# Softmax denominators of an attention kernel: four one-column fp32 matmuls replaced by two rounded 512-column matmuls and a diagonal pick, with the finish moved from tile 10 to tile 14

## The chip, the cores and the metric

The kernel runs on one core of one Trainium2 chip. The metric is the device time of one execution in microseconds (us), lower is better.

## The reference

Layer 0 is group norm and one-head self-attention over the 4096 pixels of each of 4 images with 128 channels, layer 1 a causal token attention and an 8-expert feed-forward. The change is in layer 0:

```python
    x: (4, 128, 64, 64)
    h = group_norm(x, norm_w, norm_b)                 # 32 groups
    q, k, v = h @ Wq + bq, h @ Wk + bk, h @ Wv + bv   # per pixel, 128 channels
    scores = jnp.einsum('bnc,bmc->bnm', qf, kf) * C ** (-0.5)   # N = 4096
    attn = jax.nn.softmax(scores, axis=-1)
    o = jnp.einsum('bnm,bmc->bnc', attn, vf)
    return x + (o @ Wo + bo)
```

Everything is fp32. The layer 1 part (token layer norm, a running softmax over 8 heads, top-2 of 8 experts) isn't touched.

## The kernel before

`softmax_attention` does layer 0. The queries are cut into 32 blocks of 512 (8 for each of 4 images), the keys of an image into 32 tiles of 128. The loop counter g runs over 32 x 32 = 1024 tiles: n is the block, t the tile in it, b the image and i = n % 8 the block in the image. Every engine has its own instruction stream, written out in program order; semaphores alone tie them together. For each tile TensorE computes the transposed scores of 128 keys by 512 queries (L374 to L376, three matmuls on operands split into a rounded high part and a rounded rest, type fp32r), the row scores that serve for maxima of a block 36 tiles ahead (`row_scores`, L359), and the weighted values of the tile three back (`weigh`, L388 to L390). ScalarE takes the exponential (L497, `pf`) and rounds it (L502, `p_hi`); GpSimd subtracts (`low`, L224, `p_lo`); VectorE takes maxima (L632) and adds the exponentials of a block up (L648, `sum_ps`, and the last into `den`, L652).

The sum over the 128 partitions of `den` is what the change is about. `denominators(n - 1)` is issued by TensorE at the end of the iteration t = 2 of the next block (t = 1 where i = 6): four plain fp32 matmuls, with a 128-column piece of `den` as the weights and one column of ones as the moving operand, into four columns of the shared bank `pj_ps`. VectorE's `inverse` (L657) takes the reciprocal of 128x4 values an iteration later, SyncE sends them to DRAM and back as a row broadcast over the partitions (`rb_sb`), and VectorE's `finish` (L665, L669) multiplies and adds at t = 10.

```python
for i in range(QT):
    mm = pe.matmul(pj_ps[:, i:i + 1], den[:, i * C:(i + 1) * C], ones[:, 0:1], start=True, stop=True)
mm.then_inc(den_pe, 1)
```

The bank `pj_ps` also takes the projections: `project_q` (once a block, t = 21 or 22), `project_k` for the next image (i = 6, at t = 3, 7, ..., 31), read by ScalarE's `hold_k` and VectorE's `difference` (L614 to L618) one iteration later; `project_v` (i = 7 from t = 8 on every fourth, and i = 0 at t = 0 and 4), read by `high_v` and `low_v` (L624). `key_low` (L218) on GpSimd follows at i = 7 from t = 6 on and at i = 0, t = 2. Blocks with i = 5 hold the group statistics of the next image: `channel_moments` (VectorE, t = 10), `group_means` (TensorE L257, t = 12), `group_variance` (t = 13), `scale_shift` (L697 to L701, t = 15). Block W_AT = 26 holds `weight_sums` (L705) at t = 5, 10, 15, 20 and `center_weights` (L711) one later each. Row scores stop with the block 30, t = 28.

## Time and profile before

| | |
|---|---|
| Time, median of 3 runs | 2730.43 us (2727.93 to 2730.92) |
| Time of the profiled execution | 2731.85 us, span 2730.1 us |
| TensorE busy | 2560.8 us, 94% |
| VectorE busy | 2154.0 us, 79% |
| GpSimd busy | 2059.8 us, 75% |
| ScalarE busy | 1841.1 us, 67% |
| Attention over the 32 blocks | about 65 us to 1850 us, the rest is layer 1 |
| `denominators` (L405) | 31 between 131.5 us and 1799.1 us, and a last one at 1846.8 us |

A busy TensorE isn't TensorE at its peak, since matmuls overlap in this profile: a 512-column matmul is shown as 0.39 us long, and the next one starts about 0.23 us after it. So the distance between starts is what counts. Plain fp32 matmuls show as two records each.

### The profile page before, as it was taken

To read this page: it belongs to the slowest core of one execution; us is meant where nothing else is said; L and a number is where in the kernel's file an instruction comes from. 1 tells how busy PE (TensorE), PEld (TensorE's weight loads), DVE (VectorE), ACT (ScalarE), POOL (GpSimd) and SP (SyncE) were. 2 spreads that over 40 slices of the span, in tenths; PEclk is the share of its full clock that TensorE was granted. 3 is DMA by queue.
4 is the path that set the end of the run, shared out by engine and by line. 5 is a ranking of instruction groups with operands and counts; after the bars stand their busy time and mean duration, and the time that the engine had idled before them with its cause. 6 is when DMAs were issued, how large, how long until landed. Compare 5 with 4: busy or idle time off the path is not lost. (4 is left out here: it accounts for less than half of the span.)

```text
span 2730.1 us, 37025 instructions
## 1 busy us (share of the span) xinstructions
PE 2560.8 (94%) x10851; PEld 1859.4 (68%) x10851; DVE 2154.0 (79%) x3225; ACT 1841.1 (67%) x3375; POOL 2059.8 (75%) x1688
## 2 busy tenths in 40 slices
PE   6999999999999999999999999996979999998868
PEld 2788877788887788887778888773445555555433
DVE  4788887788887788888778888861888988988984
ACT  3666777667667676667766666775877767766640
POOL 3677776777776777777677777782559989989995
PEclk7999999999999999999999999998989999999999
DMA  1000000010000010000001000101436465555645
GB/s 66 1 16 9 9 13 9 13 39 9 13 12 9 9 39 13 12 9 9 9 13 35 9 9 12 47 13 51 171 138 242 169 262 214 191 220 198 227 175 197
DMA packets 58105, 198.38 MB, mean 73 GB/s; under 512 B 12752, under 2 KB 15376, under 8 KB 40496
## 3 DMA queue, kind: packets, MB, share of 16 engines
q1 hardware_dynamic: 57904, 196.03, 20.2%
q8 instruction: 86, 1.41, 0.2%
q14 instruction: 115, 0.94, 0.1%
HBM read 178.04 MB, written 17.96 MB: 72 GB/s over the span
## 5 line engine op out<-in xcount | busy, mean ns | idle before, releaser
L224 POOL TENSOR_TENSOR p_lo<-pf,p_hi 128x512 fp32r<-128x512 f32 x1024 | 1319.8, 1292 | 433.6 <-ACT p_hi L502 431.0
L497 ACT ACTIVATE pf<-s_ps 128x512 f32<-128x512 f32 x1024 | 612.8, 598 | 530.6 <-PE s_ps L376 529.4
L632 DVE TENSOR_REDUCE mx<-m_ps 128x1 f32<-128x512 f32 x1024 | 703.0, 688 | 302.7 <-PE m_ps L359 298.7
L648 DVE TENSOR_TENSOR sum_ps<-sum_ps,pf 128x512 f32<-128x512 f32 x960 | 662.3, 690 | 21.0 <-ACT pf L497 20.7
L502 ACT CAST p_hi<-pf 128x512 fp32r<-128x512 f32 x1024 | 627.2, 613 | 0.0
L374 PE MATMUL s_ps<-q_hi,kd_hi 128*128 128x512 f32 x1024 | 427.5, 418 | 0.0
L359 PE MATMUL m_ps<-w_both,q_hi 128*128 128x512 f32 x1024 | 407.8, 401 | 11.2 <-DVE mx L632 5.4
L388 PE MATMUL om_ps<-p_hi,v_hi 128*128 128x512 f32 x1024 | 401.6, 392 | 4.6 <-POOL p_lo L224 4.6
L376 PE MATMUL s_ps<-q_lo,kd_hi 128*128 128x512 f32 x1024 | 399.8, 390 | 0.0
L375 PE MATMUL s_ps<-q_hi,kd_lo 128*128 128x512 f32 x1024 | 399.8, 390 | 0.0
L389 PE MATMUL om_ps<-p_hi,v_lo 128*128 128x512 f32 x1024 | 399.3, 390 | 0.0
L390 PE MATMUL om_ps<-p_lo,v_hi 128*128 128x512 f32 x1024 | 399.1, 390 | 0.0
L1043 POOL TENSOR_TENSOR xg<-gate_b,tv 128x512 f32<-128x512 f32 x232 | 305.7, 1325 | 41.4 <-PE mo_ps L1180 31.0
L1055 POOL TENSOR_TENSOR acc<-acc,ay 128x512 f32<-128x512 f32 x192 | 254.3, 1324 | 58.7 <-DVE ay L1375 54.3
L1180 PE MATMUL mo_ps<-xg,ew 128*128 128x512 f32 x512 | 268.9, 620 | 26.8 <-POOL xg L1043 24.3
L1375 DVE TENSOR_TENSOR_SCAN ay<-ay,carry,v_ps 128x512 f32<-128x512 f32 x224 | 286.7, 1280 | 8.7 <-DVE v_ps L1367 0.3
L1244 ACT ACTIVATE v_ps<-v_ps 128x512 f32<-128x512 f32 x256 | 149.8, 585 | 165.0 <-PE v_ps L1139 163.4
L359 PEld LDWEIGHTS m_ps<-w_both,q_hi 128*128 128x128 f32 x1024 | 194.6, 191 | 72.6 <-DVE mx L632 16.6
L1367 DVE TENSOR_TENSOR v_ps<-bq,v_ps 128x512 f32<-128x512 f32 x256 | 174.9, 683 | 85.2 <-ACT v_ps L1244 69.9
L388 PEld LDWEIGHTS om_ps<-p_hi,v_hi 128*128 128x128 f32 x1024 | 192.2, 188 | 55.3 <-POOL p_lo L224 14.1
L374 PEld LDWEIGHTS s_ps<-q_hi,kd_hi 128*128 128x128 f32 x1024 | 192.8, 188 | 50.5 <-issue 15.1
L375 PEld LDWEIGHTS s_ps<-q_hi,kd_lo 128*128 128x128 f32 x1024 | 192.8, 188 | 48.4 <-issue 12.7
(205 smaller groups left out, 3487.3 us busy)
## 6 DMA issues: line engine op xcount, KB each, us to landing
bq<-weight_rows SPq DMA_DIRECT2D x64, 1024.0 KB, 6.3
gate_b<-gate_rows SPq DMA_DIRECT2D x64, 1024.0 KB, 4.8
xb<-in_x_dram SPq DMA_DIRECT2D x8, 1024.0 KB, 6.2
rb_sb<-inverse_rows SPq DMA_DIRECT2D x32, 256.0 KB, 3.9
tokens<-xb SPq DMA_DIRECT2D x32, 256.0 KB, 2.0
tp<-tokens SPq DMA_DIRECT2D x32, 256.0 KB, 5.4
rb<-norm_rows SPq DMA_DIRECT2D x32, 256.0 KB, 5.4
tv<-tokens SPq DMA_DIRECT2D x32, 256.0 KB, 5.4
```

The source lines that it names most:

```text
L224: nc.gpsimd.tensor_tensor(p_lo[:, r, :], pf[:, r, :], p_hi[:, r, :].bitcast(F32), ALU.subtract).then_inc(lo_done, 1)
L359: pe.matmul(m_ps[:, j % 2, :], q_hi[:, n % QRING, sub * C:(sub + 1) * C], kp[:, chunk * BANK:(chunk + 1) * BANK], start=True, stop=True).t ...
L374: pe.matmul(dst, kd_hi[:, ks], q_hi[:, q, :], start=False, stop=False, skip_group_check=True)
L375: pe.matmul(dst, kd_lo[:, ks], q_hi[:, q, :], start=False, stop=False, skip_group_check=True)
L376: pe.matmul(dst, kd_hi[:, ks], q_lo[:, q, :], start=False, stop=True, skip_group_check=True).then_inc(s_pe, 1)
L388: pe.matmul(o, v_hi[:, t, :], p_hi[:, r, :], start=(t == 0), stop=False)
L389: pe.matmul(o, v_lo[:, t, :], p_hi[:, r, :], start=False, stop=False)
L390: pe.matmul(o, v_hi[:, t, :], p_lo[:, r, :], start=False, stop=(t == KT - 1)).then_inc(pv_pe, 1)
L497: nc.scalar.activation(pf[:, g % RING, :], s_ps[:, g % 2, :], ACT.Exp, scale=SCALE).then_inc(exp_done, 1)
L502: nc.scalar.copy(p_hi[:, g % RING, :], pf[:, g % RING, :]).then_inc(hi_done, 1)
L632: nc.vector.tensor_reduce(mx[:, n % 2, sub, chunk:chunk + 1], m_ps[:, j % 2, :], AX.X, ALU.max).then_inc(m_max, 1)
L648: nc.vector.tensor_tensor(sum_ps[:], sum_ps[:], p, ALU.add).then_inc(sum_done, 1)
```

## The change

For all blocks but the last, `den` is rounded on ScalarE into `den_hi` (`high_den`, at t = 2 of the next block), the rest is taken on GpSimd into `den_lo` (`low_den`, at t = 3), and TensorE multiplies a 128x128 square of ones with both, 512 columns each, adding up in `pj_ps`, at t = 5 (t = 6 where i = 0). Every partition then holds all 512 sums. VectorE multiplies the bank with the identity, repeated four times, back into `den`, sums over each 128 columns, which leaves the partition's own four values (`dsum`), and takes the reciprocal, an iteration after the matmuls. `finish` goes from t = 10 to t = 14, the experts' centring, the token statistics and their scale to later tiles, too. Who uses `pj_ps` next waits for `den_held` (the multiplication is done) and no longer for `inv_done`. The last block keeps the old form. `wv`, `wo` and `wvT` share `den`'s memory, which is used at the start alone.

```diff
-        def den_slot(i):
-            return 1 if i == NB - 2 else 2
+        def den_slot(n):
+            return 6 if n % NB == 0 else 5
...
+            def low_den(n):
+                pool.wait_ge(den_h, n + 1)
+                nc.gpsimd.tensor_tensor(den_lo[:], den[:], den_hi[:].bitcast(F32), ALU.subtract).then_inc(den_l, 1)
+
...
+                if KT <= g < TILES and g % KT == 3:
+                    low_den(g // KT - 1)
...
-                    pe.wait_ge(inv_done, n)
+                    pe.wait_ge(den_held, n if c else n - 1)
...
             def denominators(n):
-                pe.wait_ge(sum_done, (n + 1) * KT)
                 pe.wait_ge(q_l, min(n + 3, BLOCKS))
                 if n % NB == NB - 1 and n + 1 < BLOCKS:
-                    pe.wait_ge(v_l, (n // NB + 1) * CK + 7)
+                    pe.wait_ge(v_l, (n // NB + 2) * CK)
+                elif n % NB == NB - 3 and n // NB + 1 < B:
+                    pe.wait_ge(k_diff, (n // NB + 1) * CK + 1)
                 elif n % NB == NB - 2 and n // NB + 1 < B:
                     pe.wait_ge(k_diff, (n // NB + 2) * CK)
-                after(pe, inv_done, n)
+                after(pe, den_held, n)
...
-                for i in range(QT):
-                    mm = pe.matmul(pj_ps[:, i:i + 1], den[:, i * C:(i + 1) * C], ones[:, 0:1], start=True, stop=True)
-                mm.then_inc(den_pe, 1)
+                if n < BLOCKS - 1:
+                    pe.wait_ge(den_l, n + 1)
+                    pe.matmul(pj_ps[:], ones_r[:], den_hi[:], start=True, stop=False)
+                    pe.matmul(pj_ps[:], ones_r[:], den_lo[:], start=False, stop=True).then_inc(den_pe, 1)
+                else:
...
+            def high_den(n):
+                act.wait_ge(sum_done, (n + 1) * KT)
+                after(act, den_pe, n)
+                nc.scalar.copy(den_hi[:], den[:]).then_inc(den_h, 1)
...
+                    if n and t == 2:
+                        high_den(n - 1)
...
             def inverse(n):
                 dve.wait_ge(den_pe, n + 1)
                 after(dve, inv_out, 16 * (n - 1))
-                nc.vector.reciprocal(rinv[:, n % 2, :], pj_ps[:, 0:QT]).then_inc(inv_done, 1)
+                if n == BLOCKS - 1:
+                    nc.vector.reciprocal(rinv[:, n % 2, :], pj_ps[:, 0:QT]).then_inc(inv_done, 1)
+                    return
+                blocks = den[:].rearrange("p (i c) -> p i c", i=QT)
+                nc.vector.tensor_tensor(blocks, pj_ps[:].rearrange("p (i c) -> p i c", i=QT),
+                                        ident[:].unsqueeze(1).to_broadcast([C, QT, C]), ALU.mult).then_inc(den_held, 1)
+                dve.wait_ge(den_held, n + 1)
+                nc.vector.tensor_reduce(dsum[:], blocks, AX.X, ALU.add).then_inc(diag_sum, 1)
+                dve.wait_ge(diag_sum, n + 1)
+                nc.vector.reciprocal(rinv[:, n % 2, :], dsum[:]).then_inc(inv_done, 1)
...
-                    if n and t == den_slot(i) + 1:
+                    if n and t == den_slot(n) + 1:
                         inverse(n - 1)
-                    if n and t == 10:
+                    if n and t == 14:
                         finish(n - 1)
```

Line numbers of the changed kernel are a little higher (L374 becomes L379, L388 L393, L632 L651, L648 L667, L224 L225).

The first place is block 1, an ordinary block, on two engines. On TensorE the end of the iteration t = 2 was this before:

```order
L359 MATMUL m_ps<-w_both,q_hi 128x512
L388 MATMUL om_ps<-p_hi,v_hi 128x512
L389 MATMUL om_ps<-p_hi,v_lo 128x512
L390 MATMUL om_ps<-p_lo,v_hi 128x512
L405 MATMUL pj_ps<-ones,den 128x1 x4
L374 MATMUL s_ps<-q_hi,kd_hi 128x512
L375 MATMUL s_ps<-q_hi,kd_lo 128x512
```

In the changed kernel this stands at the end of the iteration t = 5:

```order
L364 MATMUL m_ps<-w_both,q_hi 128x512
L393 MATMUL om_ps<-p_hi,v_hi 128x512
L394 MATMUL om_ps<-p_hi,v_lo 128x512
L395 MATMUL om_ps<-p_lo,v_hi 128x512
L412 MATMUL pj_ps<-den_hi,ones_r 128x512
L413 MATMUL pj_ps<-den_lo,ones_r 128x512
L379 MATMUL s_ps<-q_hi,kd_hi 128x512
L380 MATMUL s_ps<-q_hi,kd_lo 128x512
```

The four one-column matmuls have become two 512-column ones and stand three tiles later.

The second is GpSimd in blocks 0 to 3, where `p_lo` is the rest of the exponentials. Before, there was nothing else until the first keys of the next image:

```order
L224 TENSOR_TENSOR p_lo<-pf,p_hi 128x512 x230
L218 TENSOR_TENSOR kd_lo<-kd,kd_hi 128x512
L224 TENSOR_TENSOR p_lo<-pf,p_hi 128x512 x4
L218 TENSOR_TENSOR kd_lo<-kd,kd_hi 128x512
L224 TENSOR_TENSOR p_lo<-pf,p_hi 128x512 x4
```

Now a `den_lo` stands after the 35th tile and then after every 32nd:

```order
L225 TENSOR_TENSOR p_lo<-pf,p_hi 128x512 x35
L229 TENSOR_TENSOR den_lo<-den,den_hi 128x512
L225 TENSOR_TENSOR p_lo<-pf,p_hi 128x512 x32
L229 TENSOR_TENSOR den_lo<-den,den_hi 128x512
L225 TENSOR_TENSOR p_lo<-pf,p_hi 128x512 x32
L229 TENSOR_TENSOR den_lo<-den,den_hi 128x512
```

Each of them stands ahead of the `p_lo` of tile 3 of its block.

The third place is VectorE in the same block (`mx` are the row maxima), t = 2 and 3 before:

```order
L632 TENSOR_REDUCE mx<-m_ps 128x1
L648 TENSOR_TENSOR sum_ps<-sum_ps,pf 128x512
L657 RECIPROCAL rinv<-pj_ps 128x4
L632 TENSOR_REDUCE mx<-m_ps 128x1
L648 TENSOR_TENSOR sum_ps<-sum_ps,pf 128x512
```

and t = 6 now:

```order
L651 TENSOR_REDUCE mx<-m_ps 128x1
L667 TENSOR_TENSOR sum_ps<-sum_ps,pf 128x512
L680 TENSOR_TENSOR den<-pj_ps,ident 128x512
L683 TENSOR_REDUCE dsum<-den 128x4
L685 RECIPROCAL rinv<-dsum 128x4
L651 TENSOR_REDUCE mx<-m_ps 128x1
L667 TENSOR_TENSOR sum_ps<-sum_ps,pf 128x512
```

Two 512-column passes came in, and the reciprocal stands behind them three tiles later. In block 6, where `kd` is the difference of keys that VectorE takes out of `pj_ps`, the same engine had this before:

```order
L657 RECIPROCAL rinv<-pj_ps 128x4
L632 TENSOR_REDUCE mx<-m_ps 128x1
L648 TENSOR_TENSOR sum_ps<-sum_ps,pf 128x512
L632 TENSOR_REDUCE mx<-m_ps 128x1
L648 TENSOR_TENSOR sum_ps<-sum_ps,pf 128x512
L614 TENSOR_SCALAR kd<-pj_ps,cols 128x256
L618 SCALAR_TENSOR_TENSOR kd<-pj_ps,cols,rb 128x256
```

and has this now:

```order
L633 TENSOR_SCALAR kd<-pj_ps,cols 128x256
L637 SCALAR_TENSOR_TENSOR kd<-pj_ps,cols,rb 128x256
L651 TENSOR_REDUCE mx<-m_ps 128x1
L667 TENSOR_TENSOR sum_ps<-sum_ps,pf 128x512
L651 TENSOR_REDUCE mx<-m_ps 128x1
L667 TENSOR_TENSOR sum_ps<-sum_ps,pf 128x512
L680 TENSOR_TENSOR den<-pj_ps,ident 128x512
L683 TENSOR_REDUCE dsum<-den 128x4
L685 RECIPROCAL rinv<-dsum 128x4
```

The denominators used the bank ahead of the first chunk of keys, and now use it behind that chunk: TensorE's two matmuls stand at the end of t = 5, and wait for the second `kd` row of t = 4.

## Rows read from the trace of the kernel before

**Rows 1.** The page: busy time, share of the span and instructions.

```profile
PE 2560.8 (94%) x10851; PEld 1859.4 (68%) x10851; DVE 2154.0 (79%) x3225; ACT 1841.1 (67%) x3375; POOL 2059.8 (75%) x1688
```

**Rows 2.** Groups by line to 2000 us: count, busy us, mean ns, idle before.

```profile
L665 DVE TENSOR_TENSOR om_ps<-om_ps,rb_sb 128x512 f32<-128x512 f32 x32 | 34.6, 1081 | 5.6 <-DMA rb_sb<-inverse_rows 5.6
...
L652 DVE TENSOR_TENSOR den<-sum_ps,pf 128x512 f32<-128x512 f32 x32 | 21.8, 681 | 1.0 <-ACT pf L497 1.0
...
L657 DVE RECIPROCAL rinv<-pj_ps 128x4 f32<-128x4 f32 x32 | 5.5, 173 | 4.4 <-PE pj_ps L405 4.2
...
L711 DVE SCALAR_TENSOR_TENSOR kd<-wsum,kd 128x512 f32<-128x512 f32 x4 | 4.7, 1168 | 0.0
L701 DVE TENSOR_TENSOR gb<-cols,gtmp 128x1 f32<-128x1 f32 x4 | 4.0, 1002 | 0.1
...
L705 DVE TENSOR_REDUCE wsum<-kd 128x4 f32<-128x512 f32 x4 | 2.7, 676 | 0.0
```

**Rows 3.** Timeline of TensorE, block 3: start us, us, engine, line.

```profile
236.06 0.39 PE L374 MATMUL s_ps<-q_hi,kd_hi 128*128 128x512 f32 x1
...
237.65 0.95 PE L405 MATMUL pj_ps<-ones,den 128*128 128x1 f32 x8
...
238.46 0.48 PE L374 MATMUL s_ps<-q_hi,kd_hi 128*128 128x512 f32 x1
...
240.13 0.39 PE L374 MATMUL s_ps<-q_hi,kd_hi 128*128 128x512 f32 x1
```

**Rows 4.** Timeline of all engines in tiles without extra work, block 4.

```profile
301.15 0.39 PE L374 MATMUL s_ps<-q_hi,kd_hi 128*128 128x512 f32 x1
...
302.26 0.69 DVE L632 TENSOR_REDUCE mx<-m_ps 128x1 f32<-128x512 f32 x1 [0.29 <-PE m_ps L359]
...
302.53 0.61 ACT L502 CAST p_hi<-pf 128x512 fp32r<-128x512 f32 x1
...
303.22 1.29 POOL L224 TENSOR_TENSOR p_lo<-pf,p_hi 128x512 fp32r<-128x512 f32 x1 [0.29 <-ACT p_hi L502]
...
304.33 0.39 PE L374 MATMUL s_ps<-q_hi,kd_hi 128*128 128x512 f32 x1
...
305.23 0.39 PE L388 MATMUL om_ps<-p_hi,v_hi 128*128 128x512 f32 x1
```

**Rows 5.** Timeline, last block: a weight load that came late.

```profile
1809.47 1.30 POOL L224 TENSOR_TENSOR p_lo<-pf,p_hi 128x512 fp32r<-128x512 f32 x1 [0.54 <-ACT p_hi L502]
...
1810.14 0.39 PE L374 MATMUL s_ps<-q_hi,kd_hi 128*128 128x512 f32 x1
...
1811.62 0.40 PE L374 MATMUL s_ps<-q_hi,kd_hi 128*128 128x512 f32 x1
```

**Rows 6.** Timeline, block 5 with the group statistics.

```profile
359.00 0.39 PE L374 MATMUL s_ps<-q_hi,kd_hi 128*128 128x512 f32 x1
...
361.04 0.39 PE L257 MATMUL pj_ps<-mom,gavg 128*128 128x2 f32 x2 [0.29 <-DVE mom L684]
...
367.39 0.64 DVE L697 TENSOR_TENSOR ga<-gst,cols 128x1 f32<-128x1 f32 x1
...
369.46 0.68 DVE L632 TENSOR_REDUCE mx<-m_ps 128x1 f32<-128x512 f32 x1
...
370.19 0.51 PE L359 MATMUL m_ps<-w_both,q_hi 128*128 128x512 f32 x1
```

**Rows 7.** Timeline, block 6 with the next image's keys.

```profile
405.71 0.39 PE L374 MATMUL s_ps<-q_hi,kd_hi 128*128 128x512 f32 x1
...
406.10 0.47 DVE L618 SCALAR_TENSOR_TENSOR kd<-pj_ps,cols,rb 128x256 f32<-128x256 f32 x1
```

**Rows 8.** Timeline of TensorE, block 8 with the last values of an image.

```profile
525.70 1.02 PE L405 MATMUL pj_ps<-ones,den 128*128 128x1 f32 x8 [0.64 <-DVE v_lo L624]
...
526.58 0.48 PE L374 MATMUL s_ps<-q_hi,kd_hi 128*128 128x512 f32 x1
```

**Rows 9.** Timeline of TensorE, block 26, the longest wait for a maximum.

```profile
1549.31 0.50 PE L359 MATMUL m_ps<-w_both,q_hi 128*128 128x512 f32 x1 [0.43 <-DVE mx L632]
```

More of the change, by code:

```diff
@@ L64, in softmax_attention @@
         shift = sb("shift", [C, 2, QB], F32R)
-        wq, wk, wv, wo = (sb(n, [C, C]) for n in ("wq", "wk", "wv", "wo"))
-        wvo, wvT = sb("wvo", [C, C]), sb("wvT", [C, C])
+        wq, wk, wvo = (sb(n, [C, C]) for n in ("wq", "wk", "wvo"))
         ident, gavg, center = both.ident, sb("gavg", [C, C]), sb("center", [C, C])
@@ L85, in softmax_attention @@
         nmax = sb("nmax", [C, 2, QT])
-        den = sb("den", [C, QB])
+        den, dsum = sb("den", [C, QB]), sb("dsum", [C, QT])
+        wv, wo, wvT = (den[:, i * C:(i + 1) * C] for i in range(3))
+        den_hi, den_lo = sb("den_hi", [C, QB], F32R), sb("den_lo", [C, QB], F32R)
         rinv = sb("rinv", [C, 2, QT])
@@ L113, in softmax_attention @@
             sem(n) for n in ("s_pe", "exp_done", "hi_done", "lo_done", "sum_done", "pv_pe"))
-        den_pe, inv_done, inv_out, on_done, t_done = (
-            sem(n) for n in ("den_pe", "inv_done", "inv_out", "on_done", "t_done"))
+        den_h, den_l, den_pe, den_held, diag_sum, inv_done, inv_out, on_done, t_done = (
+            sem(n) for n in ("den_h", "den_l", "den_pe", "den_held", "diag_sum", "inv_done", "inv_out", "on_done", "t_done"))
         rb_in = [sem(f"rb_in{i}") for i in range(2)]
@@ L255, in group_means @@
                     pe.wait_ge(q_l, (b - 1) * NB + NB - 1)
-                    pe.wait_ge(inv_done, (b - 1) * NB + NB - 3)
+                    pe.wait_ge(den_held, (b - 1) * NB + NB - 3)
                 pe.matmul(pj_ps[:, 0:2], gavg[:], mom[:], start=True, stop=True).then_inc(gn_pe, 1)
@@ L265, in project_q @@
                 else:
-                    after(pe, inv_done, n - 2)
+                    after(pe, den_held, n - 2)
                 if n >= 2 and n % NB == 0:
@@ L303, in project_v @@
                     pe.wait_ge(k_diff, (b + 1) * CK)
-                    pe.wait_ge(inv_done, n)
+                    pe.wait_ge(den_held, n)
                     if c >= 4:
                         pe.wait_ge(q_l, n + 3)
-                    if c >= 7:
-                        pe.wait_ge(inv_done, n + 1)
                 for i in range(GT):
@@ L316, in turn_weights @@
                 if g == 0:
-                    pe.wait_ge(inv_done, BLOCKS - 1)
+                    pe.wait_ge(den_held, BLOCKS - 1)
                 else:
@@ L327, in center_experts @@
                 if g == 0:
-                    pe.wait_ge(inv_done, E_AT)
+                    pe.wait_ge(den_held, E_AT)
                 else:
@@ L338, in token_means @@
                 pe.wait_ge(cst, 2)
-                pe.wait_ge(inv_done, L_AT)
+                pe.wait_ge(den_held, L_AT)
                 for a in range(B):
@@ L403, in denominators @@
                     pe.wait_ge(diff_dve, 1)
-                for i in range(QT):
-                    mm = pe.matmul(pj_ps[:, i:i + 1], den[:, i * C:(i + 1) * C], ones[:, 0:1], start=True, stop=True)
-                mm.then_inc(den_pe, 1)
+                if n < BLOCKS - 1:
[3 more added lines that the diff above has]
+                else:
+                    pe.wait_ge(sum_done, (n + 1) * KT)
+                    for i in range(QT):
+                        mm = pe.matmul(pj_ps[:, i:i + 1], den[:, i * C:(i + 1) * C], ones[:, 0:1], start=True, stop=True)
+                    mm.then_inc(den_pe, 1)
             pe.wait_ge(w_in, 160)
@@ L439, in _ @@
                         project_v(*wrapped(g, 2 * GT))
-                    if n and t == den_slot(i):
+                    if n and t == den_slot(n):
                         denominators(n - 1)
@@ L445, in _ @@
                         turn_weights(W_SLOTS.index(t - 2))
-                    if n == E_AT and t in (6, 9, 12):
-                        center_experts(t // 3 - 2)
-                    if n == L_AT and t == 5:
+                    if n == E_AT and t in (8, 11, 14):
+                        center_experts((t - 8) // 3)
+                    if n == L_AT and t == 8:
                         token_means()
-                    if n == L_AT and t == 9:
+                    if n == L_AT and t == 13:
                         token_square_means()
@@ L584, in _ @@
                         high_weights(W_SLOTS.index(t - 3))
-                    if n == E_AT and t in (7, 10, 13):
-                        hold_experts(t // 3 - 2)
+                    if n == E_AT and t in (9, 12, 15):
+                        hold_experts((t - 9) // 3)
                     if n == L_AT and 4 <= t < 4 + B:
                         square_tokens(t - 4)
-                    if n == L_AT and t == 8:
+                    if n == L_AT and t == 11:
                         square_of_means()
-                    if n == L_AT and t in (13, 15):
-                        token_scale(t // 15)
+                    if n == L_AT and t in (18, 20):
+                        token_scale(t // 20)
                     if i == NB - 3 and b + 1 < B:
@@ L650, in add @@
                     dve.wait_ge(sum_done, g)
-                    after(dve, den_pe, n)
+                    after(dve, diag_sum, n)
                     nc.vector.tensor_tensor(den[:], sum_ps[:], p, ALU.add).then_inc(sum_done, 1)
@@ L767, in _ @@
                         nc.vector.tensor_scalar(center[:], ident[:], -1.0 / C, None, ALU.add).then_inc(ctr, 1)
-                    if n == L_AT and t == 11:
+                    if n == L_AT and t == 15:
                         token_variance()
```

## The prediction, made before the changed kernel had run

> **What bounds the kernel now.** I read the page's busy times first [rows 1]: TensorE is busy for 94% of the span, the others for 67% to 79%. But a busy TensorE needn't be the limit, so I read the timeline of tiles that hold nothing extra [rows 4]. The reader is to see two things. From one L374 to the second next (301.15 to 304.33) it is 3.18 us, so a tile takes 1.59 us, which is seven matmuls at 0.227 us with no gap. And every other engine waits once a tile: VectorE 0.29 us for the row scores, GpSimd 0.29 us for `p_hi`. So in attention TensorE sets the pace, and what is taken from it shortens the kernel unless a wait takes its place. The other engines have some slack, of which two measures matter:
>
> GpSimd: the `p_lo` that starts at 303.22 ends at 304.51, and L388, which needs it, starts at 305.23 [rows 4]. That leaves 0.7 us, and a GpSimd that is late makes up 0.29 us a tile. VectorE: in block 5 a maximum started at 369.46 and ended at 370.14; the matmul that refills its bank then started at 370.19 [rows 6], just late. An undisturbed maximum starts as soon as its row scores are there [rows 4]. Its bank is refilled two tiles, 3.18 us, after those began; they take 0.39 us like every 512-column matmul here and the maximum 0.69 us, which leaves about 2.0 us. So VectorE may be 2.0 us behind before TensorE waits, and makes up 0.29 us a tile.
>
> A wait costs more than its length. In the last block six matmuls should take 1.36 us; where `p_lo` ended at 1810.77, only 0.05 us before its matmul was due, the tile took 1.48 us [rows 5]. The weights are loaded one matmul ahead, and that load had waited. I count 0.12 us for each late release.
>
> **The change part by part.** *Matmuls.* L374 to the second next L374 across the old denominators takes 240.13 - 236.06 = 4.07 us [rows 3]; less 3.18 us they cost 0.89 us. The new ones are two of the 0.227 us kind, 0.45 us. Gross 0.44 us in each of 31 blocks, 13.6 us in all. The last block keeps the old form.
>
> *Waiting for `den_lo`.* ScalarE is busy for two thirds of the time [rows 1], and the copy (0.61 us like its cast, [rows 4]) fits the free part of a tile but for 0.1 us. GpSimd's subtraction has L224's shape, 1.29 us. It follows the `p_lo` of tile 2. By [rows 4] that `p_lo` ends 0.7 us before the L388 of its tile, the subtraction ends 0.6 us after that L388 starts, and the new matmuls are due three matmuls after it, at 0.68 us. So `den_lo` comes within 0.1 us of the moment it is due: the weight load is late, the matmul hardly. I count 0.12 us. The `p_lo` of tile 3 is 1.29 - 0.29 = 1.0 us late, TensorE is 0.45 + 0.12 us later too, and the rest is inside the 0.7 us. An ordinary block so saves 0.89 - 0.45 - 0.12 = 0.32 us. There are 20 such (i = 1 to 4 of images 0 to 2, i = 7 of the same, and blocks 25, 27 to 30): 6.4 us.
>
> *VectorE.* The multiplication reads one operand from PSUM and one from SBUF: 0.68 us like L652, or 1.08 us like L665, whose layout is turned. Blocks of 128 aren't turned, so I take 0.68. The reduction is 0.68 us like L705, the reciprocal 0.17 us like L657 [rows 2]. Together 1.53 us at t = 6. Less 0.29 this is 1.24 us behind, gone by t = 11; the finish at t = 14 (L665's 1.08 us and a second pass, 1.8 us in all) comes on top of nearly nothing. Both stay under 2.0, so in ordinary blocks it costs nothing. If VectorE had no slack, it would cost 1.36 us a block.
>
> *Block i = 5 (three times).* Before, the finish at t = 10 stood ahead of `channel_moments`, and L257 came at 361.04 behind it [rows 6]; by the pace it was due at 359.00 + 1.59 = 360.59, so with the refill 0.57 us are lost. With the finish at t = 14 this wait goes. But then VectorE has 1.8 us of finish at t = 14 and the scale and shift at t = 15, which took 369.46 - 367.39 = 2.07 us [rows 6]; with what is left over from t = 10 and 13 it is 3.7 us behind, 1.7 over. That costs 1.8 us; before, L359 at 370.19 was only just late, for some 0.3 us. Net per block 0.32 + 0.57 - 1.5 = -0.6 us, three times -1.9 us.
>
> *Block i = 6 (three times).* The first keys are projected at t = 3, and their last `kd` ends at 406.10 + 0.47 = 406.57. The new matmuls are due at the end of t = 5, which is where L374 stood at 405.71 [rows 7]. They wait 0.92 us, 1.03 with the refill, and I add 0.2 us for the second chunk, due just as the multiplication ends. So 0.89 becomes 0.45 + 1.03 + 0.2 = 1.7: -0.8 us, three times -2.4 us.
>
> *Block i = 0 (three times).* The denominators waited 0.64 us for `v_lo` [rows 8], and cost 0.89 + 0.64 + 0.12 = 1.65 us. At t = 6 they wait for nothing like it, but GpSimd has `key_low` at t = 2 and `den_lo` at t = 3 in a row: 2.58 us, less 0.58 made up, 0.9 from the `project_v` at t = 4 (eight matmul records like the old denominators, 0.89 us) and 0.7 of slack, is 0.4 us; ScalarE's and the weight load's share may double it. I take 0.9 us. Now 1.65, then 0.45 + 0.9: +0.3 us, three times +0.9 us.
>
> *Block 26.* Weight sums and centring are 0.68 and 1.17 us on VectorE [rows 2], two pairs between t = 5 and 11 and one beside the finish at 14. Work from t = 5 to 16 is 3 x 1.85 + 1.8 + 1.53 = 8.9 us, against 11 x 0.29 + 0.45 + 2.0 = 5.6 us: 3.3 us waited for, where before, without the 1.53 us, L359 waited 0.43 us once and its weight load longer [rows 9], some 0.9 us in all. Net 0.32 - 3.3 + 0.9 = -2.1 us.
>
> *Block 31.* TensorE has six matmuls a tile and GpSimd little slack (1.29 in 1.36 us); the 1.29 us takes the place of nearly all that the matmuls give. +0.3 us.
>
> Layer 1 behind it is unchanged; tokens' statistics are later in block 30 but still done before it ends. SyncE's queue waits for `inv_done` three tiles later and for the finish four later, with 8 tiles (12.7 us) between, for two transfers that now hide in 7.
>
> **Sum.** 6.4 - 1.9 - 2.4 + 0.9 - 2.1 + 0.3 = 1.2 us saved. The profiled execution took 2731.85 us, so it would take 2730.6; that one stands 1.4 us above the median of 2730.43, so I forecast 2729.2 us. What a measurement of this kernel can tell from no change is about 0.2%, 5.5 us.
>
> Bounds: `den_lo` early enough for no late load, +2.4 us, or one load more late in each block, -2.4 us; L665's 1.08 us for the multiplication, 0.4 us in each of the four crowded blocks, -1.6 us; VectorE's sums in those blocks a third off, +-2.5 us. That gives 2724 to 2736.
>
> **The rivals.** *The gains come whole.* If VectorE and the bank have more room than I count, nothing is given back: 31 x 0.44 = 13.6 us, 2716.8 us. For it speaks that TensorE waits for VectorE only seldom now, against it the two crowded blocks where it already does. 0.16.
>
> *The reciprocal waits for GpSimd; this one ends slower.* It now reads SBUF, not PSUM. L701, a one-column operation of VectorE on SBUF, took 1.00 us on average, six times the four-column reciprocal's 0.17 [rows 2], which looks like the length of a GpSimd instruction (1.29 us). If the reciprocal waits as long, 1.1 us more, VectorE is 2.35 us behind in each ordinary block: 0.46 us each, 9.2 us, and 4.4 us more in the crowded four: 2742.8 us. It decides from 0.76 us of waiting on. Against it: it has one operand, L701 two. The Trainium skill, "SBUF — State Buffer", section "Who interferes with whom", says that VectorE and GpSimd share a port pair which an instruction holds whole, that two SBUF inputs, copies, casts and `tensor_scalar` contend for it, and that a reduction doesn't; it doesn't name the reciprocal. By that list this rival falls; the 1.00 us of L701 agrees with its part on two inputs. 0.08.
>
> *`den_lo` is later than I count*, by 0.3 us, as ScalarE's copy or GpSimd's order delays it: 20 x 0.3 = 6 us, 2735.2 us. 0.14.
>
> **How the numbers follow.** My forecast has 0.62, the others 0.16, 0.08 and 0.14. The range 2721 to 2738 leaves out most of the first rival and all of the second. Faster by over 0.2%: the first rival and a little of the forecast, 0.2. Slower: the second, half of the third and a little of the forecast, 0.18. Within: 0.62.
>
> **What would show it.** L374 to the second next across the new matmuls should be 3.18 + 0.57 us. In blocks 5, 13, 21 L359 should wait near 1.7 us for `mx` and L257 not at all; in 6, 14, 22 the new matmuls should wait some 0.9 us for `kd`; in block 26 some 3 us for `mx`. The reciprocal should be 0.17 us. A `p_lo` waited for in ordinary blocks, or no wait in the crowded ones, makes me wrong.

## The result and the profile after

| | before | after |
|---|---|---|
| Median | 2730.68 us (2727.63 to 2736.91, 20 runs) | 2724.43 us (2716.27 to 2729.03, 20 runs) |
| Profiled execution | 2731.85 us, span 2730.1 us | 2728.70 us, span 2726.9 us |

The ratio is 0.9973, with a 95% interval of 0.9965 to 0.9981: the medians lie 6.25 us apart, where 1.2 us was forecast. That is just past the 0.2%, or 5.5 us, that the prediction took as the least that can be told from nothing. The two profiled executions, which all traces below come from, lie 3.15 us apart.

The page's busy times, which answer to [rows 1]:

```profile
PE 2555.4 (94%) x10665; PEld 1840.3 (67%) x10665; DVE 2189.6 (80%) x3287; ACT 1857.4 (68%) x3406; POOL 2098.9 (77%) x1719
```

They say little: three engines got busier and the kernel got faster. Since TensorE sets the pace, I read how long it takes for each block, from the start of the first L374 of a block (L379 now) to that of the next block's. This table is worked out from TensorE's timeline; block 31 is read up to the start of its last tile. In blocks 5, 6 and 8 and their like the three blocks of a kind agree within 0.1 us. Of the 20 ordinary ones 14 read as block 2; the other six (1, 7, 15, 23, 27 and 30) hold other work as well and are longer, up to 61 us, but change alike: all 20 changes lie between -0.28 and -0.38 us.

| Block | How many | Before | After | Change | Forecast |
|---|---|---|---|---|---|
| ordinary, as block 2 | 20 | 53.09 | 52.73 | -0.35 | -0.32 |
| i = 5, as block 5 | 3 | 54.60 | 54.03 | -0.57 | +0.6 |
| i = 6, as block 6 | 3 | 63.85 | 64.45 | +0.60 | +0.8 |
| i = 0, as block 8 | 3 | 56.48 | 55.97 | -0.51 | -0.3 |
| block 26 | 1 | 53.93 | 54.42 | +0.49 | +2.1 |
| block 31 | 1 | 47.11 | 47.58 | +0.47 | -0.3 |

Together 31 blocks of attention take 7.29 us less. What lies ahead of block 1 took 2.7 us longer in this execution and layer 1 took 1.4 us longer; the sums are in neither. Layer 1's time, from the last L379 to the end of the span, lay between 885.5 and 901.0 us in the twelve kernels that were profiled here, all with the same layer 1. So stretches that the edit doesn't touch scatter by more than the edit changes, and that is why the block table, not the total, decides about edits of a few us.

The groups by line of the changed kernel's trace, up to 2000 us, for the operations that are new (count, busy us, mean ns, idle before), answer to [rows 2]:

```profile
L229 POOL TENSOR_TENSOR den_lo<-den,den_hi 128x512 fp32r<-128x512 f32 x31 | 40.2, 1297 | 0.0
L683 DVE TENSOR_REDUCE dsum<-den 128x4 f32<-128x512 f32 x31 | 21.3, 687 | 1.1
L680 DVE TENSOR_TENSOR den<-pj_ps,ident 128x512 f32<-128x512 f32 x31 | 21.1, 681 | 0.6 <-PE pj_ps L413 0.6
L519 ACT CAST den_hi<-den 128x512 fp32r<-128x512 f32 x31 | 19.3, 623 | 0.0
...
L412 PE MATMUL pj_ps<-den_hi,ones_r 128*128 128x512 f32 x31 | 14.0, 453 | 2.8 <-issue 2.4 <-POOL den_lo L229 0.4
...
L685 DVE RECIPROCAL rinv<-dsum 128x4 f32<-128x4 f32 x31 | 5.5, 178 | 1.1
```

Every duration is the one that was taken from a like row of before: 1.30 for 1.29, 0.68 for 0.68, 0.18 for 0.17. The new matmuls waited 2.8 us in all: three times 0.81 us in blocks 6, 14 and 22, and 0.35 us in block 31. In the other 27 blocks they didn't.

An ordinary tile with the new matmuls, block 2, all engines (start us, us), answers to [rows 3]:

```profile
190.12 0.39 PE L379 MATMUL s_ps<-q_hi,kd_hi 128*128 128x512 f32 x1
...
190.26 1.30 POOL L229 TENSOR_TENSOR den_lo<-den,den_hi 128x512 fp32r<-128x512 f32 x1
...
191.67 0.19 PEld L412 LDWEIGHTS pj_ps<-den_hi,ones_r 128*128 128x128 f32 x1 [0.22 <-issue]
191.71 0.46 PE L412 MATMUL pj_ps<-den_hi,ones_r 128*128 128x512 f32 x1
...
192.01 0.40 PE L413 MATMUL pj_ps<-den_lo,ones_r 128*128 128x512 f32 x1
192.24 0.40 PE L379 MATMUL s_ps<-q_hi,kd_hi 128*128 128x512 f32 x1
```

The tile takes 2.12 us, which is 1.59 + 0.53; 0.57 was forecast. `den_lo` ends at 191.56 and L412 starts at 191.71, 1.59 us after the tile began: on time. But its weights (the LDWEIGHTS row) are loaded only from 191.67, 0.41 us after the load before them, where 0.23 is usual. L412 shows 0.46 us and L413 follows 0.30 us later instead of 0.23: the late weight load, at 0.07 us and not 0.12.

Block 5, all engines, with the group statistics, which answers to [rows 6]:

```profile
359.98 0.39 PE L379 MATMUL s_ps<-q_hi,kd_hi 128*128 128x512 f32 x1
...
361.56 0.28 PE L264 MATMUL pj_ps<-mom,gavg 128*128 128x2 f32 x2
...
369.43 0.52 DVE L725 TENSOR_TENSOR ga<-gst,cols 128x1 f32<-128x1 f32 x1
...
370.17 0.16 DVE L729 TENSOR_TENSOR gb<-cols,gtmp 128x1 f32<-128x1 f32 x1
...
370.22 1.28 POOL L225 TENSOR_TENSOR p_lo<-pf,p_hi 128x512 fp32r<-128x512 f32 x1 [0.29 <-PE om_ps L395]
370.25 0.68 DVE L651 TENSOR_REDUCE mx<-m_ps 128x1 f32<-128x512 f32 x1
...
370.99 0.50 PE L364 MATMUL m_ps<-w_both,q_hi 128*128 128x512 f32 x1
```

L264 starts 1.58 us into its tile and has no wait left, as forecast. But the last two operations of `scale_shift` (L725 and L729, L697 and L701 before) take 0.82 us with the one between them, from L725's start to the next maximum's (L651, 370.25), and not 2.07 us as in [rows 6].

The trace of before shows why it had been 2.07 us (the same place, all engines):

```profile
368.23 1.29 POOL L224 TENSOR_TENSOR p_lo<-pf,p_hi 128x512 fp32r<-128x512 f32 x1 [0.23 <-ACT p_hi L502]
368.25 1.28 DVE L701 TENSOR_TENSOR gb<-cols,gtmp 128x1 f32<-128x1 f32 x1
```

A one-column operation of two SBUF inputs lasted 1.28 us, started 0.02 us behind GpSimd's and ended with it. Blocks 13 and 21 read the same (816.55 to 817.83 us beside 816.52 to 817.81). Now it starts 0.05 us ahead of GpSimd's and takes 0.16 us. VectorE comes to it at another moment since the finish stands at t = 14. That the finish does this is shown by experiment 5, which puts it back at t = 10: the three operations take 1.26 to 1.28 us again, started 0.02 to 0.05 us behind GpSimd's. In all ten traces with the finish at t = 14, 30 places, they take 0.16 us.

### The profile page after: what moved, and what is told of

Same layout as the page of the kernel before. It is cut to its first block and busy times, and to the rows that moved or that the text cites. A ratio compares the mean times of both kernels' runs of the same rounds, so it can differ in the third digit from the quotient of the medians.

```text
span 2726.9 us, 36807 instructions
## 1 busy us (share of the span) xinstructions
PE 2555.4 (94%) x10665; PEld 1840.3 (67%) x10665; DVE 2189.6 (80%) x3287; ACT 1857.4 (68%) x3406; POOL 2098.9 (77%) x1719
## 3 DMA queue, kind: packets, MB, share of 16 engines
q8 instruction: 85, 1.39, 0.2%
## 5 line engine op out<-in xcount | busy, mean ns | idle before, releaser
L225 POOL TENSOR_TENSOR p_lo<-pf,p_hi 128x512 fp32r<-128x512 f32 x1024 | 1321.4, 1295 | 388.0 <-ACT p_hi L514 385.5
L651 DVE TENSOR_REDUCE mx<-m_ps 128x1 f32<-128x512 f32 x1024 | 701.3, 686 | 264.6 <-PE m_ps L364 257.5
L667 DVE TENSOR_TENSOR sum_ps<-sum_ps,pf 128x512 f32<-128x512 f32 x960 | 661.5, 689 | 20.1 <-ACT pf L509 19.6
L379 PE MATMUL s_ps<-q_hi,kd_hi 128*128 128x512 f32 x1024 | 424.8, 415 | 0.0
L364 PE MATMUL m_ps<-w_both,q_hi 128*128 128x512 f32 x1024 | 408.3, 401 | 12.1 <-DVE mx L651 6.1
L393 PE MATMUL om_ps<-p_hi,v_hi 128*128 128x512 f32 x1024 | 402.0, 393 | 6.2 <-POOL p_lo L225 6.2
L364 PEld LDWEIGHTS m_ps<-w_both,q_hi 128*128 128x128 f32 x1024 | 194.5, 191 | 76.3 <-DVE mx L651 19.4
L393 PEld LDWEIGHTS om_ps<-p_hi,v_hi 128*128 128x128 f32 x1024 | 192.1, 188 | 58.5 <-POOL p_lo L225 17.7
L379 PEld LDWEIGHTS s_ps<-q_hi,kd_hi 128*128 128x128 f32 x1024 | 192.7, 188 | 51.8 <-issue 15.1
```

The costliest lines, as they stand in the source:

```text
L225: nc.gpsimd.tensor_tensor(p_lo[:, r, :], pf[:, r, :], p_hi[:, r, :].bitcast(F32), ALU.subtract).then_inc(lo_done, 1)
L364: pe.matmul(m_ps[:, j % 2, :], q_hi[:, n % QRING, sub * C:(sub + 1) * C], kp[:, chunk * BANK:(chunk + 1) * BANK], start=True, stop=True).t ...
L379: pe.matmul(dst, kd_hi[:, ks], q_hi[:, q, :], start=False, stop=False, skip_group_check=True)
L393: pe.matmul(o, v_hi[:, t, :], p_hi[:, r, :], start=(t == 0), stop=False)
L651: nc.vector.tensor_reduce(mx[:, n % 2, sub, chunk:chunk + 1], m_ps[:, j % 2, :], AX.X, ALU.max).then_inc(m_max, 1)
L667: nc.vector.tensor_tensor(sum_ps[:], sum_ps[:], p, ALU.add).then_inc(sum_done, 1)
```

## The experiments

The first eight edits are made to the changed kernel; the ninth joins the seventh and the eighth, and the tenth adds one edit to the ninth. Block times are read as in the table above.

**1. The old sums at the new places.** Four plain matmuls and the plain reciprocal, but at t = 5, with the finish at t = 14.

```diff
-                if n < BLOCKS - 1:
-                    pe.wait_ge(den_l, n + 1)
-                    pe.matmul(pj_ps[:], ones_r[:], den_hi[:], start=True, stop=False)
-                    pe.matmul(pj_ps[:], ones_r[:], den_lo[:], start=False, stop=True).then_inc(den_pe, 1)
-                else:
...
+                pe.wait_ge(sum_done, (n + 1) * KT)
+                for i in range(QT):
+                    mm = pe.matmul(pj_ps[:, i:i + 1], den[:, i * C:(i + 1) * C], ones[:, 0:1], start=True, stop=True)
```

> The four one-column fp32 matmuls and the plain reciprocal are back, at the changed kernel's places (t = 5, or 6 where i = 0) and with its finish at t = 14; no den_hi, den_lo or diagonal. My theory, that the 0.35 us of an ordinary block are matmul starts alone: an ordinary block takes 53.09 us again (it was 52.73 in the changed kernel); block 5 about 54.0 us, since the finish no longer stands ahead of the group statistics; block 8 about 55.7; block 6 about 64.8, since the wait for the bank stays and the longer matmuls come back; the whole about 1 us under the kernel before. The rival, that the places and the later finish bring the gain and not the form of the sums: 52.7 us for an ordinary block, and 6 us under the kernel before in all.

2732.58 us beside 2732.91 of before, ratio 0.9995 (0.9983 to 1.0007). Block 2 takes 53.09 us, as before; block 31 takes 47.10. TensorE's timeline of block 2:

```profile
187.54 0.39 PE L377 MATMUL s_ps<-q_hi,kd_hi 128*128 128x512 f32 x1
...
189.12 0.95 PE L410 MATMUL pj_ps<-ones,den 128*128 128x1 f32 x8
...
189.93 0.48 PE L377 MATMUL s_ps<-q_hi,kd_hi 128*128 128x512 f32 x1
```

So the gain of the ordinary blocks is the matmuls' form alone, and the move is worth nothing there. In the others the move takes and gives: block 6 takes 65.00 us (+1.15), block 8 takes 55.85 (-0.63), block 5 takes 54.39 (-0.20); over 31 blocks +0.75 us. Block 5 had been expected at 54.0; its 54.39 is the changed kernel's 54.03 and the 0.36 us of the old form.

**2. The rest one tile earlier**, to give the weight load its time.

```diff
-                if KT <= g < TILES and g % KT == 3:
+                if KT <= g < TILES and g % KT == 2:
...
-                    if n and t == 2:
+                    if n and t == 1:
```

> The changed kernel with the rounding of den at t = 1 and the subtraction on GpSimd at t = 2, one tile earlier; the matmuls stay at t = 5. The iteration with them takes 2.12 us in the changed kernel, 0.53 over the pace where two matmul starts are 0.45. My theory, that the 0.08 us is a weight load that waits for den_lo: 2.04 us, and 31 x 0.08 = 2.5 us less in all, and in block 31 the 0.35 us wait for den_lo gone. The rival, that any pair of matmuls with waits ahead of it costs 0.08 us more: 2.12 us still, and a total within 0.5 us of the changed kernel but for block 31.

2734.60 us, ratio 1.0005 (0.9992 to 1.0017). The expectation failed: attention takes 11 us more than in the changed kernel, where 2.5 us less had been expected. Block 2 takes 53.06 us. Its tile t = 5 (all engines), which begins at 188.41:

```profile
186.96 1.30 POOL L229 TENSOR_TENSOR den_lo<-den,den_hi 128x512 fp32r<-128x512 f32 x1
...
188.21 3.81 POOL L225 TENSOR_TENSOR p_lo<-pf,p_hi 128x512 fp32r<-128x512 f32 x3
...
189.56 0.19 PEld L393 LDWEIGHTS om_ps<-p_hi,v_hi 128*128 128x128 f32 x1 [0.50 <-POOL p_lo L225]
...
190.36 0.40 PE L412 MATMUL pj_ps<-den_hi,ones_r 128*128 128x512 f32 x1
...
190.60 0.39 PE L413 MATMUL pj_ps<-den_lo,ones_r 128*128 128x512 f32 x1
...
190.83 0.39 PE L379 MATMUL s_ps<-q_hi,kd_hi 128*128 128x512 f32 x1
```

The pair itself is now free of the late load: 190.36 to 190.83 is 0.47 us. But the `p_lo` behind `den_lo` is late, and the weight load of `weigh` waits 0.50 us for it; the tile takes 2.42 us, 0.36 more than its seven matmuls and the pair. In the changed kernel the `p_lo` behind `den_lo` is that of tile 3, which `weigh` takes at t = 6, when TensorE has just spent 0.53 us more on the sums; here it is that of tile 2, taken at t = 5 ahead of them.

**3. and 4. A second pass on VectorE**, to ask whether VectorE has the slack that I counted: the multiplication twice (3), and a second multiplication with both inputs in SBUF (4).

```diff
+                                        ident[:].unsqueeze(1).to_broadcast([C, QT, C]), ALU.mult).then_inc(den_first, 1)
+                dve.wait_ge(den_first, n + 1)
+                nc.vector.tensor_tensor(blocks, pj_ps[:].rearrange("p (i c) -> p i c", i=QT),
```

```diff
+                nc.vector.tensor_tensor(blocks, blocks,
```

> The changed kernel with VectorE's multiplication done twice, both times out of pj_ps (one input in PSUM): 0.68 us more on VectorE at t = 6 of 31 blocks, same values. My theory, that VectorE may be 2.0 us behind before TensorE waits: 1.24 + 0.65 = 1.9 us behind, so an ordinary block stays at 52.73 us or gains one late load of 0.1; blocks 5 and 26 pay, some 0.5 us each. The rival, that VectorE's work at t = 6 is already on the path: 0.65 us in each block, 20 us in all.

> The changed kernel with a second multiplication on VectorE, of den with the identity, both inputs in SBUF; the values don't change. It is there to measure what the small operations of the group statistics met. If an operation of VectorE with two inputs in SBUF waits for the GpSimd instruction that runs: it takes from 0.68 to 2.0 us instead of 0.68, VectorE falls 2.4 us or more behind at t = 6 and an ordinary block takes 0.5 us or more longer than in the run with both inputs' first in PSUM. If it doesn't wait: 0.68 us, and the same blocks as in that run.

The third took 2730.07 us and the fourth 2732.24, one run each. With the third, 0.68 us more of VectorE's time in each block leaves the ordinary blocks at 52.73 to 52.77 us: there the slack is real. Block 6 takes 65.25 (+0.80), since the next key projection waits longer for the bank. Blocks 5 and 26, where I had expected 0.5 us each, read 54.06 and 54.43, the changed kernel's own times. In block 5 the added pass comes well ahead of the finish. Block 26 has no such room, as TensorE waits 0.54 us for a maximum at t = 9 there as it does in the changed kernel. What gave way is the centring, `kd<-wsum,kd`, which reads two inputs in SBUF. All engines, the changed kernel and then the third:

```profile
1534.45 1.29 POOL L225 TENSOR_TENSOR p_lo<-pf,p_hi 128x512 fp32r<-128x512 f32 x1 [0.30 <-ACT p_hi L514]
...
1534.65 1.65 DVE L739 SCALAR_TENSOR_TENSOR kd<-wsum,kd 128x512 f32<-128x512 f32 x1
...
1536.22 0.68 DVE L651 TENSOR_REDUCE mx<-m_ps 128x1 f32<-128x512 f32 x1
```

```profile
1534.99 1.29 POOL L226 TENSOR_TENSOR p_lo<-pf,p_hi 128x512 fp32r<-128x512 f32 x1 [0.29 <-ACT p_hi L515]
...
1535.91 0.92 DVE L743 SCALAR_TENSOR_TENSOR kd<-wsum,kd 128x512 f32<-128x512 f32 x1
```

It starts 0.20 us after GpSimd's `p_lo` in the first and 0.92 us after it in the third, and ends 0.55 us after the end of that `p_lo` in both. So the pass filled time that the centring would have spent waiting for GpSimd.

The fourth takes 0.17 us more in an ordinary block, not the 0.5 expected. Its second pass, all 31 (min/median/max ns):

```profile
L684 DVE TENSOR_TENSOR den<-den,ident x31: 872/879/1445, 138.9 to 1803.4; 128x512 f32<-128x512 f32 x31
```

0.88 us beside 0.68 of the form that reads PSUM. It starts while a GpSimd instruction runs (one from 190.88 to 192.18 us, the pass from 191.84 to 192.72) and ends 0.54 us after that one does. Only 0.34 us of GpSimd's instruction were left when it started, so it waited little; in block 31, where 0.90 us were left, it took 1.45 us. So two SBUF inputs do wait for GpSimd, and how long depends on the moment.

**5. The finish back at t = 10.**

```diff
-                    if n and t == 14:
+                    if n and t == 10:
```

> The changed kernel with the finish back at t = 10, the rest as it is. From the last block before the change, the reciprocals need 5.6 us to come back as rows; in the changed kernel they are ready about 4.8 us before VectorE would reach the finish at t = 10. My theory, that the later finish is needed by the later sums: VectorE waits 0.8 us for rb_sb, is 2.3 us behind with the finish, and an ordinary block takes 53.1 us, as before the change, the whole gain gone; block 5 more than 54.6. The rival, that the place of the finish doesn't matter in ordinary blocks: 52.73 us.

2750.92 us, one run. Attention takes 22 us more than in the changed kernel; those that were 52.73 us take 53.07 to 54.01 us, block 5 55.78, block 8 59.73. One finish on VectorE in block 2:

```profile
200.07 1.07 DVE L693 TENSOR_TENSOR om_ps<-om_ps,rb_sb 128x512 f32<-128x512 f32 x1 [0.74 <-DMA rb_sb<-inverse_rows]
```

Behind it stand VectorE's maxima. For the line's 32 instances the waits for the broadcast are 20.4 us in all (17 times), and 5.6 us in the changed kernel (once, in the last block, as in [rows 2]). So the later finish is no extra: reciprocals that come three tiles later need it.

**6. The high part alone.** No `den_lo` and one matmul. The sums lose the part that `den_hi` rounds away.

```diff
             def low_den(n):
-                pool.wait_ge(den_h, n + 1)
-                nc.gpsimd.tensor_tensor(den_lo[:], den[:], den_hi[:].bitcast(F32), ALU.subtract).then_inc(den_l, 1)
+                pass
...
+                    pe.matmul(pj_ps[:], ones_r[:], den_hi[:], start=True, stop=True).then_inc(den_pe, 1)
```

> The changed kernel without the rest of den: no subtraction on GpSimd and one matmul of 512 columns in place of two, so that the sums are those of the rounded values. It shows what GpSimd's 1.29 us cost. My theory: nothing in an ordinary block but the 0.08 us late weight load, so 52.73 - 0.23 - 0.08 = 52.42 us; but in block 31, where a tile is six matmuls and GpSimd nearly fills it, the 0.35 us wait and what follows go too, under 47.0 us instead of 47.58; in block 8 the wait for p_lo at t = 6, 0.8 us, goes with it. The rival, that GpSimd's part is free everywhere: 0.23 us less in each block and no more.

2721.06 us, one run; 52.44 us for block 2 and 46.70 for block 31. TensorE in block 2:

```profile
182.45 0.39 PE L378 MATMUL s_ps<-q_hi,kd_hi 128*128 128x512 f32 x1
...
184.04 0.40 PE L411 MATMUL pj_ps<-den_hi,ones_r 128*128 128x512 f32 x1
...
184.28 0.40 PE L378 MATMUL s_ps<-q_hi,kd_hi 128*128 128x512 f32 x1
```

One matmul takes 0.24 us and nothing is late. Against the changed kernel that is 0.29 us an ordinary block, which is the second matmul and the late load. Block 31 gets 0.88 us back and block 8 0.80, far over the matmul's 0.24: the other 0.64 and 0.56 us are what GpSimd's subtraction cost, the late load with them.

**7. The rest in halves**, one at t = 2 and one at t = 3, with the rounding at t = 1, so that GpSimd is never 1.3 us late at once.

```diff
+                for part in parts:
+                    sl = slice(part * HALF, (part + 1) * HALF)
+                    nc.gpsimd.tensor_tensor(den_lo[:, sl], den[:, sl], den_hi[:, sl].bitcast(F32), ALU.subtract).then_inc(den_l, 1)
...
+                if KT <= g < TILES and g % KT in (2, 3):
+                    low_den(g // KT - 1, (g % KT - 2,))
```

> The changed kernel with the rounding at t = 1 and GpSimd's subtraction in two halves of 256 columns, one at t = 2 and one at t = 3. The run with all of it at t = 2 lost 0.37 us at the p_lo of tile 2 and won the 0.08 us of the late weight load. A 128x256 subtraction is 0.73 us on GpSimd, so the p_lo of tile 2 is 0.44 us late, inside the 0.65 us margin, and den_lo is done 0.15 us sooner than in the changed kernel. My theory: the iteration t = 5 takes 2.05 us instead of 2.12, an ordinary block 52.66, and attention is 2 us shorter than in the changed kernel. The rival, that the margin is smaller than I read it: 2.2 us or more for that iteration, and slower than the changed kernel.

2724.30 us, ratio 0.9971 (0.9961 to 0.9981). Ordinary blocks take 52.67 us, the late load gone, as expected. But block 8 takes 56.64 (+0.67), where half of `den_lo` now lies ahead of `key_low` and `weigh` waits for a late `p_lo` at three tiles in a row. That eats the gain: attention takes 0.7 us more than in the changed kernel, where 2 us less had been expected.

**8. The old sums where it is crowded.** The rounded form in ordinary blocks and i = 5; the old matmuls and plain reciprocal for the denominators that are due in blocks with i = 6 (at t = 1, ahead of the first keys), i = 0 (at t = 6) and block 31.

```diff
         def den_slot(n):
-            return 6 if n % NB == 0 else 5
+            if n == BLOCKS - 1:
+                return 2
+            return 6 if n % NB == 0 else 1 if keys_next(n) else 5
...
+        def plain(n):
+            return n >= BLOCKS - 2 or keys_next(n + 1) or n % NB == NB - 1
...
-                if n < BLOCKS - 1:
+                if not plain(n):
...
-                if n == BLOCKS - 1:
+                if plain(n):
```

> The changed kernel with the old four one-column matmuls and the plain reciprocal in the blocks i = 6 that project keys (at t = 1 again, ahead of the keys), in i = 0 (at t = 6) and in block 31 (at t = 2); the rounded sums elsewhere; the finish at t = 14 everywhere. My theory, block by block: 63.9 us instead of 64.5 for i = 6, since the wait for kd goes; 55.85 instead of 56.0 for i = 0, as in the run with the old sums at the new places; 47.1 instead of 47.6 for block 31; so attention is 2.6 us shorter than in the changed kernel and 9 to 10 us shorter than before. The rival, that these blocks' losses come from the finish at t = 14 and not from the sums' place: 64.5 and 47.6 as they are.

2717.89 us, ratio 0.9948 (0.9934 to 0.9961). Blocks 6, 8 and 31 take 63.81, 55.83 and 47.10 us, and attention 3.1 us less than in the changed kernel, 10.4 less than before. In block 6, on TensorE, nothing is waited for:

```profile
391.01 0.95 PE L426 MATMUL pj_ps<-ones,den 128*128 128x1 f32 x8
```

**9. and 10. Both together, and the weight sums spread.** The ninth is 8 with the halves of 7. The tenth moves block 26's `weight_sums` to t = 0, 10, 20, 26 (and `center_weights` one later), so that none stands near the diagonal pick or the finish.

```diff
+    SUM_SLOTS = (0, 10, 20, 26)
...
-                    if n == W_AT and t in W_SLOTS:
-                        weight_sums(W_SLOTS.index(t))
+                    if n == W_AT and t in SUM_SLOTS:
+                        weight_sums(SUM_SLOTS.index(t))
```

> Both that helped in one: the old sums in the blocks i = 6 that project keys, in i = 0 and in block 31, and in the others the rounded ones with GpSimd's subtraction in halves at t = 2 and t = 3. If the two gains are independent: 52.67 us for an ordinary block, 63.85, 55.82 and 47.1 for the crowded ones, so attention is 1.4 us (23 x 0.06) shorter than in the run with the old sums alone, near 2716.5 us in all. If they aren't: as that run, 2717.9.

> The same with VectorE's weight sums and centring of block 26 at t = 0, 10, 20 and 26 (and one later) in place of 5, 10, 15 and 20, away from the diagonal at t = 6 and the finish at t = 14. Block 26 took 54.4 us in the changed kernel, 1.7 over an ordinary one. My theory, that this is VectorE more than 2.0 us behind at two places (0.83 us each in the changed kernel's trace): both go, and block 26 takes under 53.2 us, 1.2 us or more off. The rival, that the work itself is too much for the block, wherever it stands: 54.4 us.

The ninth: 2720.63 us beside 2730.48, ratio 0.9963 (0.9950 to 0.9975). Ordinary blocks 52.69 us, but attention only 0.35 us less than in the eighth, not the 1.4 expected; 17 of the 20 ordinary blocks take 0.04 to 0.06 us less, which gives 0.7, but blocks 7, 15 and 23 take 0.08 to 0.12 us more and block 31 0.11. Blocks 7, 15 and 23 scatter that much between runs, so more can't be read from it. The tenth: 2717.40 us, ratio 0.9947 (0.9932 to 0.9963), the best version here, 5.6 us of attention under the changed kernel and 12.90 under before. Block 26 went from 54.38 to 52.72 us, within 0.05 us of what an ordinary block takes. Eight and ten can't be told apart by their medians; their block tables can.

## Why the prediction was right, and where it wasn't

The measured time, 6.25 us under before, is inside the range and 5 us under the number. The mechanism was the forecast's: the matmuls gain, and crowded blocks give a part back. The sizes in the crowded blocks were not. Five of the six terms were too pessimistic, by 6.9 us together, and one was too optimistic, by 0.8. The range held because it was 17 us wide; for the blocks with i = 5 and 26 alone the error was 5.2 us, twice the 2.5 us that the bounds allowed there. And 6.25 us is past the 5.5 us that bounded the likeliest case: it fell where the prediction had put 0.2, mainly for the first rival.

**What held.** *Matmuls:* 0.42 us gross in an ordinary block (53.09 to 52.67, experiment 7), 0.44 forecast. Experiment 1 gives the old form 53.09 us at either place, 6 has one rounded matmul at 0.24 us, 2 and 7 the pair at 0.47. *Late load:* right in kind, 0.07 us and not 0.12, so 20 ordinary blocks gave 7.0 us, not 6.4. *VectorE's slack in ordinary blocks:* shown by 3, which adds 0.68 us for at most 0.04. *Block i = 6:* the wait for `kd` was 0.81 us, 0.92 forecast (406.57 - 405.71 in [rows 7] is 0.86; no row shows the other 0.06). Block 6 of the changed kernel, all engines, answers to [rows 7]:

```profile
405.98 0.47 DVE L637 SCALAR_TENSOR_TENSOR kd<-pj_ps,cols,rb 128x256 f32<-128x256 f32 x1
...
406.56 0.47 PE L412 MATMUL pj_ps<-den_hi,ones_r 128*128 128x512 f32 x1 [0.81 <-issue]
...
407.09 0.39 PE L379 MATMUL s_ps<-q_hi,kd_hi 128*128 128x512 f32 x1
```

The profile calls the wait "issue", but `kd` ends at 406.45, 0.11 us before L412 starts, and where these sums stand ahead of the keys (8) it is gone. *Block i = 0:* -0.51 for -0.3; the tile t = 6 takes 2.82 us, which is 1.59 + 0.45 and 0.78 for the 0.9 forecast; `weigh` waits 0.49 us of it for `p_lo`, and without `den_lo` (6) the tile takes 2.02. *The reciprocal:* 177 to 179 ns in all 31 instances, so the rival by which it waits for GpSimd is false. The Trainium skill, "SBUF — State Buffer", section "Who interferes with whom", says in general that a VectorE instruction with at most one SBUF input doesn't contend with GpSimd, outside its two-port modes; the reciprocal is one, and the trace agrees.

**What failed: block i = 5**, the step "the scale and shift at t = 15, which took 2.07 us ... it is 3.7 us behind, 1.7 over. That costs 1.8 us". The size of `scale_shift` was taken from a row in which L701 held 1.28 us for a one-column operation. I had seen that number, and used it against the reciprocal, but counted it here as work. It was a wait for GpSimd, and a wait doesn't move with its instruction. The 2.07 us became 0.82; then VectorE is 3.7 - 1.25 = 2.45 us behind, 0.45 over, and the two stalls after it (t = 17 and 18) are 0.68 us together, 0.34 more than before; the weights of L364 wait 0.39 and 0.56 us for `mx` there, where near 1.7 was to be the sign. With the wait of L257 gone (0.56) and the ordinary 0.35, that is -0.57, as measured. Where 1.9 us were to be lost in the three blocks, 1.7 were won: 3.6 of the 6.1 us between the forecast sum (1.2) and the trace (7.3). The short L729 goes with the place of the finish in all twelve traces: 1.26 to 1.28 us in the two with the finish at t = 10 (before and 5), 0.16 us in the ten others.

**Block 26** (+0.49 for +2.1), the step "8.9 us, against 11 x 0.29 + 0.45 + 2.0". TensorE in block 26, which answers to [rows 9]:

```profile
1536.95 0.50 PE L364 MATMUL m_ps<-w_both,q_hi 128*128 128x512 f32 x1 [0.55 <-DVE mx L651]
...
1553.66 0.50 PE L364 MATMUL m_ps<-w_both,q_hi 128*128 128x512 f32 x1 [0.48 <-DVE mx L651]
```

Some 3 us of waiting was to be the sign; there are two stalls of this size, at t = 9 and 19, and the tiles there are 0.83 us longer; before it was 0.10 and 0.73. One is at t = 19, behind the finish and the third pair, not within my window of t = 5 to 16. I summed the work of eleven tiles against one allowance, as if the backlog only grew; a tile-by-tile account is needed. That VectorE's queue is the cause is shown by 10, where spreading its work takes 1.66 us away, both stalls. And a part of that queue is waiting once more: the 1.17 us of the centring [rows 2] is a mean of 0.69 to 1.39 us, and in the changed kernel its four instances take 1.65, 0.68, 1.25 and 0.69, each of them ending 0.55 us after a `p_lo` on GpSimd.

**Block 31** (+0.47 for -0.3). All engines:

```profile
1797.63 1.28 POOL L229 TENSOR_TENSOR den_lo<-den,den_hi 128x512 fp32r<-128x512 f32 x1
...
1799.06 0.47 PE L412 MATMUL pj_ps<-den_hi,ones_r 128*128 128x512 f32 x1 [0.35 <-POOL den_lo L229]
```

The step "takes the place of nearly all" was too mild: with the form's 0.44 us gained and 0.47 lost, the new waits cost 0.91 us, twice the gain, and 0.64 of them go with `den_lo` (6).

By terms: 20 x -0.35 - 1.7 + 2.0 - 1.6 + 0.5 + 0.5 = -7.3 us of attention. The first rival, that the gains come whole at 13.6 us, is false for this kernel. Experiment 10 comes near its number (12.90), but by other ways: it uses the new form in 24 blocks only, some 0.4 us each, or 9.6 us, and the other 3.3 are waits of the kernel before that went with the new places (0.66 in each block with i = 0, 0.2 in each with i = 5, 0.8 in block 26). Of the 6.3 us between 13.6 and 7.3, the blocks with i = 6 hold 3 x 1.1 = 3.3, blocks 26 and 31 0.9 each, and the ordinary blocks 20 x 0.09 = 1.8, most of it the late load; the others gained a little over 0.44 each. The third rival, `den_lo` late, shows only in block 31.

## What to carry to other kernels

Before a duration from a trace goes into a sum, ask whether it is work or waiting: an instruction whose mean is several times that of its smallest like is waiting inside, and it may be free at the new place. Where a rewrite makes an instruction cheaper on one engine and spends the others' slack, apply it only where that slack is there; keeping the old form in seven of 31 blocks was worth 3.1 us beside a change of 7.3. And when the program's other parts scatter by more than the edit, measure the stretch that it touches: equal blocks agreed here within 0.1 us, while the totals of one kernel spread over as much as 16.
